# Splitting the routed experts' down weights once per expert, ahead of the expert loop, and taking their projection in fp32r

## The chip, the cores and the metric

One NeuronCore of a Trainium2 chip runs the whole kernel, as one program. The metric is the device time of one execution in microseconds (us). The kernel before takes 1118.25 us in the median of 3 runs (1118.01 to 1118.48).

## The reference, cut to what matters

```python
# B, S, D = 2, 1024, 512; T = B*S tokens; 16 heads of 32; 8 experts, inner width F = 352, top 2
def ref(x, Wq, Wk, Wv, Wo, router, bias, gate, up, down, sgate, sup, sdown):
    xn = layernorm(x)
    # causal attention, softmax, then the output projection
    Q, K, V = heads(xn @ Wq.T), heads(xn @ Wk.T), heads(xn @ Wv.T)
    A = softmax(where(causal, Q @ K.T / sqrt(32), -1e30)) @ V
    attn = merge(A) @ Wo.T
    # mixture of experts over the T tokens of xn: top 2 of 8, group-limited
    cw = combine_weights(sigmoid(xn @ router.T), bias)       # [T, 8], two non-zero per row
    routed = sum(cw[:, e:e+1] * (silu(xn @ gate[e].T) * (xn @ up[e].T)) @ down[e].T
                 for e in range(8))
    shared = (silu(xn @ sgate.T) * (xn @ sup.T)) @ sdown.T   # inner width 704
    return x + attn + routed + shared
```

## The kernel before, in words

Everything is float32. A product that is to be exact to float32 is taken in one of two ways. Either the operands stay float32, and each product takes two weight loads and two matmul records. Or each operand is split into a high part (a copy in fp32r) and a low part (the operand less its high part, again in fp32r), and three fp32r products are summed: high by high, high by low, low by high. All large products use the second way but one, the routed down projection.

The program is a sequence of blocks with a barrier between them:

1. `norm_phase` and `project_phase` (to about 210 us): layernorm, V, Q and K, the router.
2. `attend_phase` (to about 760 us): 32 heads (batch by head), each cut into 12 steps, written out in full (no loop on the chip). Every engine walks the same list of steps s = 0, 1, 2, ... and does for each step the stages whose lag fits. The scores for block s are taken at step s + 24 on TensorE (L1458), the exponential in the same step on ScalarE (`exp`, L1236) and its high part one step later (`hi`, L1243), the low part at step s + 26 (`lo`), on GpSimd for ten of a head's twelve blocks (L1198) and on VectorE for blocks 4 and 8 (L1325), and the product with V at step s + 30 (L1481, L1483). `prob` has four buffers, so `exp` of block s waits for `lo` of block s - 4; `ps_s` has two, so the scores of block s wait for `exp` of block s - 2. The shared expert's matmuls (L1514, L1539) are spread between the attention's as filler, so that every step has about equal TensorE work (`fill_counts`).
   SyncE (queue SP) loads for this phase in one loop over heads, `for g in range(HEADS + 4)`: `next_head(g)`, which first waits for the scores of head g - 4 and then issues 6 loads (L188, L190); for some g `load_xt` (one load of 2048 KB, L995; g = 3, 6, 11, 16, 20, 25, 30), or `store_acc` (4 stores of 256 KB, L1012) followed by `load_base` (L1006), which waits until those stores have landed and then issues 4 loads (g = 4, 8, 13, 17, 22, 27, 32; the first loads, at g = 1, have no store before them); then `load_values(g - 1)` (L989); then raw pieces of the shared expert's second half into `gu_raw` and `d_raw` (L1019 and the like, for g up to 15).
   GpSimd also works out where each token's row goes among the routed slots (`place()`: `expert_of`, `slot_table`), one small instruction a step.
3. `out_phase` (760 to 820 us): 16 token tiles, attention output by Wo, added to `out`. SP loads `wo` into the end of `d_sb`, a tile of `out` per step, and, at tiles 1 and 8, all weights of experts 0 and 1 with `load_expert` (L209, L212, L214).
4. `routed_phase` (820 us to the end): 39 tiles of 128 token slots, sorted by expert, so that an expert has some 5 tiles. On TensorE a tile j is worked on in three steps of a software pipeline, `pipeline(pe, NST, U, [(0, turn_x), (2, turn_h), (1, gate_up), (2, down)])`: transposes of the gathered rows (`ps_xt`, L1883), transposes of the hidden values of tile j - 2 (`ps_ht`, L1906), 24 fp32r matmuls for gate and up of tile j - 1 (L1895), and the down projection of tile j - 2 in float32 (L1916). ScalarE makes the high parts of the rows (L1797) and of the gate and up weights, once per tile and four chunks each (L1806), and the SiLU (L1819). VectorE makes the low parts (L1854, L1862), the hidden product (L1831), copies the transposed hidden values (L1839, L1841) and scales the result (L1847). GpSimd gathers rows (L1768) and adds results to `out` with an indirect DMA (L1779), one after the other. Each engine that needs the expert's number reads it with a load to a register (L1747). SP loads the remaining experts two ahead.

The change touches `attend_phase` (the SP loop, `place`, the GpSimd stream), `load_expert`, `out_phase` (where `wo` lies, the first loads) and `routed_phase` (all streams). New are `load_down`, `downs_loaded`, `load_down_raw`, `store_down_parts` and `split_down`.

## Time and profile before

| what | value |
|---|---|
| median of 3 runs | 1118.25 us |
| the profiled execution, its own time | 1127.01 us |
| span of the profiled execution (first to last instruction) | 1125.0 us |
| TensorE (PE) busy | 1046.2 us (93%) |
| VectorE (DVE) | 784.6 us (70%) |
| ScalarE (ACT) | 637.9 us (57%) |
| GpSimd (POOL) | 506.4 us (45%) |
| mean granted TensorE clock | 0.969 of full |
| DMA | 163.61 MB, mean 145 GB/s |

How to read it: the profile is of one execution, which took 8.8 us longer than the median of the runs without a profile. Busy time of PE counts modelled ends of pipelined matmuls; the pace of a run of matmuls is read from their starts. PEld is TensorE's weight load, which runs beside the matmuls.

### The profile page before, as it was taken

The page shows a single profiled execution, that of the slowest core. Times are in us where ns is not written, and L with a number is a line of the kernel's source. Part 1 is how long each engine was busy: PE and PEld are TensorE (multiplying, and loading weights), DVE is VectorE, ACT ScalarE, POOL GpSimd, SP SyncE. Part 2 cuts the span into 40 slices and gives each one's busy share as a digit, 9 for nine tenths or more (in the row PEclk, how much of TensorE's full clock was granted, in tenths as well). Part 3 has the DMA queues.
Part 4 walks back from the last instruction along what each step waited for, and adds up shares of the span by engine and source line. Part 5 has one row for each costly group of instructions (what it writes and reads, how often), then busy time and mean ns, then how long its engine had stood idle before and what let it go on. Part 6 is the DMA issues. An engine that isn't in the chain of part 4 may idle for free. (4 is left out here: it accounts for less than half of the span.)

```text
span 1125.0 us, 18890 instructions
## 1 busy us (share of the span) xinstructions
PE 1046.2 (93%) x5379; PEld 817.6 (73%) x5380; DVE 784.6 (70%) x1675; ACT 637.9 (57%) x1278; POOL 506.4 (45%) x568
## 2 busy tenths in 40 slices
PE   6999979888899998999999999998989999999994
PEld 4767867666677776777778777776867777778872
DVE  6732324565688887788888888865568888888872
ACT  3323211265588786787787887872155555565550
POOL 0013903388756564556566565651013443333321
PEclk9999989988899999999999999998989999999997
DMA  6989996255543553644445426118789444443432
GB/s 213 322 335 361 136 293 231 94 67 102 132 133 77 150 148 75 163 118 136 115 113 151 126 64 191 45 39 266 243 283 278 90 76 75 75 72 68 71 54 35
DMA packets 106201, 163.61 MB, mean 145 GB/s; under 512 B 53984, under 2 KB 64480, under 8 KB 102656
## 3 DMA queue, kind: packets, MB, share of 16 engines
q1 hardware_dynamic: 95776, 141.82, 44.1%
q0 software_dynamic: 9760, 20.49, 10.0%
q8 instruction: 38, 0.62, 0.2%
q14 instruction: 51, 0.42, 0.1%
q10 hardware_dynamic: 576, 0.26, 0.1%
HBM read 101.25 MB, written 61.28 MB: 144 GB/s over the span
## 5 line engine op out<-in xcount | busy, mean ns | idle before, releaser
L1198 POOL TENSOR_TENSOR prob_lo<-prob,prob_hi 128x512 fp32r<-128x512 f32 (+2 forms) x320 | 308.3, 977 | 203.3 <-ACT prob_hi L1243 147.0
L1236 ACT ACTIVATE prob<-ps_s 128x512 f32<-128x512 f32 (+3 forms) x384 | 188.0, 490 | 127.1 <-PE ps_s L1463 77.1
L1243 ACT ACTIVATE prob_hi<-prob 128x512 fp32r<-128x512 f32 (+3 forms) x384 | 198.6, 517 | 12.4 <-ACT row_stage L1217 12.4
L1862 DVE TENSOR_TENSOR rw_lo<-gu_sb,rw_hi 128x704 fp32r<-128x704 f32 x156 | 138.8, 893 | 52.7 <-ACT rw_hi L1806 47.7
L1306 DVE CUSTOM_DVE_ANT_0 ps_m<-ps_m,causal 128x384 f32<-128x384 f32 (+3 forms) x256 | 126.7, 495 | 69.2 <-PE ps_m L1432 66.9
L1806 ACT ACTIVATE rw_hi<-gu_sb 128x704 fp32r x156 | 123.5, 794 | 62.8 <-PE ps_ru L1895 43.6
L1458 PE MATMUL ps_s<-qs,ks 97*128 97x512 f32 (+3 forms) x384 | 140.4, 366 | 9.4 <-ACT prob L1236 9.2
L1779 POOL DMA_INDIRECT out<-work,slot_table x39 | 63.5, 1627 | 181.1 <-DVE work L1847 148.2
L1481 PE MATMUL ps_o<-prob_hi,vs 128*66 128x512 f32 (+3 forms) x384 | 133.1, 347 | 10.4 <-issue 9.6
L1432 PE MATMUL ps_m<-ks,qs 96*128 96x512 f32 (+3 forms) x384 | 139.1, 362 | 0.6 <-DVE maxima L1306 0.2
L1483 PE MATMUL ps_o<-prob_lo,vs 128*66 128x512 f32 (+3 forms) x384 | 132.0, 344 | 0.0
L1310 DVE TENSOR_REDUCE maxima<-ps_m 128x1 f32<-128x512 f32 x128 | 85.8, 682 | 41.5 <-PE ps_m L1432 40.4
L1916 PE MATMUL ps_ry<-d_sb,work 128*128 (+1 forms) x234 | 106.9, 593 | 1.2 <-issue 1.2
L1458 PEld LDWEIGHTS ps_s<-qs,ks 97*128 97x128 f32 x384 | 74.8, 195 | 30.8 <-ACT prob L1236 15.9
L1432 PEld LDWEIGHTS ps_m<-ks,qs 96*128 96x128 f32 x384 | 74.3, 193 | 23.6 <-DVE maxima L1306 4.6
L613 PE MATMUL ps_q<-xt,w_hi 128*128 128x512 f32 x256 | 82.0, 398 | 6.4 <-DVE work L725 6.4
L1481 PEld LDWEIGHTS ps_o<-prob_hi,vs 128*66 128x66 f32 x384 | 54.3, 141 | 32.1 <-issue 21.4
L725 DVE TENSOR_TENSOR work<-ps_q,work 128x512 fp32r<-128x512 f32 x32 | 21.8, 690 | 78.8 <-ACT work L574 76.9
L1514 PE MATMUL ps_f<-xt,sg_hi 128*128 128x512 f32 (+1 forms) x192 | 70.5, 400 | 3.8 <-PEq L496 2.7
L1514 PE MATMUL ps_f<-xt,su_hi 128*128 128x512 f32 (+1 forms) x192 | 71.5, 406 | 0.0
L1916 PEld LDWEIGHTS ps_ry<-d_sb,work 128*128 128x128 f32 (+1 forms) x234 | 43.4, 190 | 38.7 <-issue 38.7
L1768 POOL DMA_INDIRECT work<-xn_rows,slot_table x35 | 37.5, 1073 | 58.8 <-PE ps_xt L1883 48.7
(201 smaller groups left out, 2353.0 us busy)
## 6 DMA issues: line engine op xcount, KB each, us to landing
xt<-xt_blocks SPq DMA_DIRECT2D x7, 2048.0 KB, 9.1
v_rows<-work SPq DMA_DIRECT2D x16, 512.0 KB, 3.0
xt_blocks<-xt SPq DMA_DIRECT2D x4, 2048.0 KB, 11.3
qk_hi<-work SPq DMA_DIRECT2D x8, 1024.0 KB, 4.7
qk_lo<-work SPq DMA_DIRECT2D x8, 1024.0 KB, 7.5
qs<-qk_hi SPq DMA_DIRECT2D x64, 128.0 KB, 2.9
ks<-qk_hi SPq DMA_DIRECT2D x64, 128.0 KB, 3.2
vs<-v_rows SPq DMA_DIRECT2D x32, 256.0 KB, 4.7
```

The source lines that it names most:

```text
L1198: nc.gpsimd.tensor_tensor(prob_lo[:, s % NPL, 0:w], prob[:, s % NP, 0:w], prob_hi[:, s % NPH, 0:w].bitcast(F32), ALU.subtract).then_inc(lo ...
L1236: nc.scalar.activation(prob[:, s % NP, 0:w], ps_s[s % NS][:, 0:w], ACT.Exp, scale=SCALE).then_inc(exp_done, 1)
L1243: nc.scalar.activation(prob_hi[:, s % NPH, 0:w], prob[:, s % NP, 0:w], ACT.Copy).then_inc(hi_ready, 1)
L1306: nc.vector.tensor_tensor_reduce(ps_m[s % NM][:, 0:w], ps_m[s % NM][:, 0:w], causal[:, TBW - w:], 1.0, MASKED, ALU.add, ALU.max, maxima[:, ...
L1432: nc.tensor.matmul(ps_m[s % NM][:, 0:w], qs[0:ROWS, c, t * P:(t + 1) * P], ks[0:ROWS, c, k0:k0 + w], start=True, stop=True).then_inc(m_don ...
L1458: last = nc.tensor.matmul(ps_s[s % NS][:, 0:w], ks[0:ROWS + 1, c, kt * P:(kt + 1) * P], qs[0:ROWS + 1, c, q0:q0 + w], start=True, stop=not ...
L1481: nc.tensor.matmul(into, vs[:, c, kt, :], prob_hi[:, s % NPH, 0:w], start=n in STARTS, stop=False)
L1483: nc.tensor.matmul(into, vs[:, c, kt, :], prob_lo[:, s % NPL, 0:w], start=False, stop=n in ENDS).then_inc(pv_done, 1)
L1514: last = nc.tensor.matmul(ps_f[part][0:w, :], (w_hi, w_lo, w_hi)[term][:, kc, f0:f0 + w], xt[:, (0, 0, 1)[term], kc, :], start=(j == 0), s ...
L1806: nc.scalar.activation(w_hi[:, k, :], chunk(e, k), ACT.Copy).then_inc(w_hi_ready, 1)
L1862: nc.vector.tensor_tensor(w_lo[:, k, :], chunk(e, k), w_hi[:, k, :].bitcast(F32), ALU.subtract).then_inc(w_lo_ready, 1)
L1916: last = nc.tensor.matmul(ps_y[c % 2][:, :], hid_t[0:w, c % HR, k, :], d_sb[0:w, bass.ds(e * NF + k, 1), :].rearrange("p a d -> p (a d)"), ...
```

## The change

The down weights of the eight experts are cut into 24 pieces (8 experts by chunks of 128, 128 and 96 rows of 512). From head 18 of the SP loop on, two pieces a head (g = 18 to 29; `SPLIT_FROM` works out to 18) are loaded into `d_raw`; GpSimd makes the high part of each (a copy, into `gu_raw`) and the low part (a subtraction, in place), and SP stores both to a new DRAM tensor `down_split`. In the expert loop the split weights of an expert, twice as many bytes, are loaded into a ring of four places; the down projection takes nine fp32r matmuls a tile in place of three float32 ones; the hidden values are split on ScalarE (high) and VectorE (low); the scaling moves from VectorE to ScalarE. `place()` gets five more small instructions.

```diff
@@ attend_phase
+    SPLITS = E * NF
+    SPLIT_FROM = head_after(max(DOWN_SPLIT_AT) + 1)
+    MAKE_AT = {NB * (SPLIT_FROM + i // 2 - 1) + 5 + 3 * (i % 2): i for i in range(SPLITS)}
@@ SP
+                def load_down_raw(i):
+                    (e, k), n = divmod(i, NF), i % SR
+                    f0, w = FCH[k]
+                    if i < SR:
+                        sp.wait_ge(d_lo_ready, NF)
+                    wait(sp, parts_stored[n], stored_before + 32 * (i // SR))
+                    sp.dma_start(d_raw[0:w, n, :], down[e, f0:f0 + w, :]).then_inc(w_loaded[n], 16)
+                def store_down_parts(i):
+                    (e, k), n = divmod(i, NF), i % SR
+                    w = FCH[k][1]
+                    sp.wait_ge(down_made, 2 * i + 1)
+                    sp.dma_start(down_dram[e, 0:w, 0, k, :],
+                                 gu_raw[0:w, i % 2].rearrange("p k q -> p (k q)")
+                                 ).then_inc(parts_stored[n], 16)
+                    sp.wait_ge(down_made, 2 * i + 2)
+                    sp.dma_start(down_dram[e, 0:w, 1, k, :], d_raw[0:w, n, :]
+                                 ).then_inc(parts_stored[n], 16)
                 for g in range(HEADS + 4):
                     if HS <= g < HEADS:
                         next_head(g)
+                    i = 2 * (g - 1 - SPLIT_FROM)
+                    if 0 <= i < SPLITS:
+                        store_down_parts(i)
+                        store_down_parts(i + 1)
...
                         if g == DOWN_RAW_AT[k]:
                             load_shared_down(k)
+                    i = 2 * (g - SPLIT_FROM)
+                    if 0 <= i < SPLITS:
+                        load_down_raw(i)
+                        load_down_raw(i + 1)
@@ GpSimd
+                def split_down(s):
+                    if s in MAKE_AT:
+                        i = MAKE_AT[s]
+                        n, w = i % SR, FCH[i % NF][1]
+                        pool.wait_ge(w_loaded[n], raw_before + 16 * (i // SR + 1))
+                        if i >= 2:
+                            pool.wait_ge(parts_stored[(i - 2) % SR],
+                                         stored_before + 32 * ((i - 2) // SR + 1))
+                        into = gu_raw[0:w, i % 2].rearrange("p k q -> p (k q)")
+                        nc.gpsimd.tensor_copy(into.bitcast(F32R), d_raw[0:w, n, :]
+                                              ).then_inc(down_made, 1)
+                    if s - 1 in MAKE_AT:
...
+                        nc.gpsimd.tensor_tensor(d_raw[0:w, n, :], d_raw[0:w, n, :],
+                                                gu_raw[0:w, i % 2].rearrange("p k q -> p (k q)"),
+                                                ALU.subtract).then_inc(down_made, 1)
-                steps([(LO, lo)])
+                for s in range(max(ALL, max(MAKE_AT) + 2)):
+                    if 0 <= s - LO < STEPS:
+                        lo(s - LO)
+                    split_down(s)
@@ out_phase
-        wo_raw = d_sb[:, E * len(FCH) - KC:, :]
+        wo_raw = gu_sb[:, (E - 1) * KC:, 0:D]
-                        load_expert(sp, e, gate, up, down, gu_sb, d_sb, expert_loaded)
+                        load_expert(sp, e, gate, up, gu_sb, expert_loaded)
+                        load_down(sp, e, down_dram, d_ring, down_loaded)
@@ routed_phase, SP: experts 4 to 7 of the ring
+                for e in range(DOWN_SLOTS, E):
+                    first = sp.value_load(first_of[0:1, e - DOWN_SLOTS + 1:e - DOWN_SLOTS + 2],
+                                          min_val=1, max_val=NST + 1)
+                    sp.wait_ge(y_ready, first)
+                    load_down(sp, e, down_dram, d_ring, down_loaded)
+                    sp.wait_ge(down_loaded[e % DOWN_SLOTS], downs_loaded(e))
+                    sp.sem_inc(downs_ready, 1)
@@ routed_phase, ScalarE
+                def hidden_hi(i, c):
...
+                    nc.scalar.activation(hid_hi[:, c % HR, 0:2, :], ps_h[:, 0:2, :], ACT.Copy
+                                         ).then_inc(h_hi_ready, 1)
+                    nc.scalar.activation(hid_hi[0:w, c % HR, 2, :], ps_h[0:w, 2, :], ACT.Copy
+                                         ).then_inc(h_hi_ready, 1)
+                def weigh(i, c):
...
+                    nc.scalar.activation(y[:, c % R, :], ps_y[c % 2][:, :], ACT.Copy,
+                                         scale=slot_table[:, bass.ds(j, 1), 1]).then_inc(y_ready, 1)
-                pipeline(act, NST, U, [(0, turn_x), (0, first_chunks), (1, gate_unit), (0, last_chunk)],
+                pipeline(act, NST, U, [(0, turn_x), (3, weigh), (2, hidden_hi), (0, first_chunks),
+                                       (1, gate_unit), (0, last_chunk)], back=R)
@@ routed_phase, VectorE
+                def hidden_lo(i, c):
...
+                    nc.vector.tensor_tensor(hid_lo[:, c % HR, 0:2, :], ps_h[:, 0:2, :],
+                                            hid_hi[:, c % HR, 0:2, :].bitcast(F32), ALU.subtract)
+                    nc.vector.tensor_tensor(hid_lo[0:w, c % HR, 2, :], ps_h[0:w, 2, :],
+                                            hid_hi[0:w, c % HR, 2, :].bitcast(F32), ALU.subtract)
-                pipeline(dve, NST, U, [(4, turn_h), (2, x_lo), (2, first_chunks),
-                                       (3, hidden), (2, last_chunk), (4, weigh)], back=U)
+                pipeline(dve, NST, U, [(0, x_lo), (2, hidden_lo), (0, first_chunks),
+                                       (1, hidden), (0, last_chunk)], back=U)
@@ routed_phase, TensorE
                 def down(i, c):
                     e = expert(pe, j)
-                    pe.wait_ge(experts_ready, e + 1)
+                    n = pe.value_load(down_slot[0:1, bass.ds(j, 1)], min_val=0,
+                                      max_val=DOWN_SLOTS - 1)
+                    pe.wait_ge(downs_ready, e + 1)
                     wait(pe, h_ready, 2 * (j + 1))
-                    wait(pe, y_ready, j - 1)
+                    wait(pe, y_ready, j)
                     for k, (f0, w) in enumerate(FCH):
-                        last = nc.tensor.matmul(
-                            ps_y[c % 2][:, :], hid_t[0:w, c % HR, k, :],
-                            d_sb[0:w, bass.ds(e * NF + k, 1), :].rearrange("p a d -> p (a d)"),
-                            start=(k == 0), stop=(k == NF - 1))
+                        for of, part in ((hid_hi, 0), (hid_hi, 1), (hid_lo, 0)):
+                            last = nc.tensor.matmul(
+                                ps_y[c % 2][:, :], of[0:w, c % HR, k, :],
+                                d_ring[0:w, bass.ds(n, 1), part * NF + k, :]
+                                .rearrange("p a d -> p (a d)"),
...
```

## Rows read from the trace of the kernel before

**Rows 1.** Windows, a head and the loop: us, busy PE PEld DVE ACT POOL, PEclk, DMA.

```profile
613.07:628.55 15.48, 15.48 (x90) 12.43 (x89) 12.81 (x35) 12.41 (x28) 9.49 (x11) 1.00 0.31 69
...
830.00:1125.00 295.00, 277.96 (x1417) 219.18 (x1415) 221.74 (x343) 160.26 (x227) 98.51 (x72) 0.98 0.48 101
```

**Rows 2.** Chain of waits, one tile of the expert loop: start us, us, what.

```profile
1003.34 2.58 PE ps_ry L1916 x6
1005.92 0.44 PE ps_xt L1883 x4
...
1010.56 0.86 PE ps_ry L1916 x2
```

**Rows 3.** Timeline of ACT and DVE in that tile: start us, us, instruction.

```profile
1011.48 0.52 DVE L1831 TENSOR_TENSOR work<-ps_ru,work 128x352 f32<-128x352 f32 x1
1011.55 0.79 ACT L1806 ACTIVATE rw_hi<-gu_sb 128x704 fp32r x1 [0.49 <-issue]
```

**Rows 4.** Timeline of PE in the output projection, eight matmuls apart.

```profile
785.17 0.39 PE L1697 MATMUL ps_ay<-wo_hi,a_hi 128*128 128x512 f32 x1
...
787.01 0.39 PE L1697 MATMUL ps_ay<-wo_hi,a_lo 128*128 128x512 f32 x1
```

**Rows 5.** Groups by form of POOL: busy us, mean ns | idle before.

```profile
L1198 POOL TENSOR_TENSOR prob_lo<-prob,prob_hi 128x512 fp32r<-128x512 f32 x128 | 166.3, 1312 | 68.9 <-ACT prob_hi L1243 67.3 <-PE ps_o L1483 0.4
...
L705 POOL CAST sd_hi<-sd_raw 96x512 fp32r<-96x512 f32 x1 | 0.7, 671 | 0.0
```

**Rows 6.** Groups by form of DVE, one that reads two SBUF operands.

```profile
L1352 DVE TENSOR_TENSOR o_sum<-o_part 128x128 f32<-128x128 f32 x64 | 41.1, 643 | 0.0
```

**Rows 7.** Timeline of POOL, blocks 2 and 3, then 5, of the head at 628.55.

```profile
634.96 1.44 POOL L1198 TENSOR_TENSOR prob_lo<-prob,prob_hi 128x384 fp32r<-128x384 f32 x2 [0.67 <-ACT prob_hi L1243]
638.77 0.74 POOL L1198 TENSOR_TENSOR prob_lo<-prob,prob_hi 128x256 fp32r<-128x256 f32 x1 [2.37 <-ACT prob_hi L1243]
```

**Rows 8.** Timeline of ACT and PE: exponential of block 9, scores of block 11.

```profile
641.71 0.28 ACT L1236 ACTIVATE prob<-ps_s 128x128 f32<-128x128 f32 x1 [0.34 <-PE ps_s L1463]
...
643.97 0.45 PE L1458 MATMUL ps_s<-qs,ks 97*128 97x512 f32 x1
```

**Rows 9.** Timeline of SP's issues in two heads.

```profile
597.86 0.31 SPq L188 DMA_DIRECT2D qs<-qk_hi  x1
...
601.81 0.43 SPq L989 DMA_DIRECT2D vs<-v_rows  x1
...
628.55 0.30 SPq L188 DMA_DIRECT2D qs<-qk_hi  x1
...
638.01 0.43 SPq L989 DMA_DIRECT2D vs<-v_rows  x1
```

**Rows 10.** Line L989, window 601 to 603: its DMA to landing.

```profile
DMA to landing us min/median/max: 8.8/8.8/8.8
```

**Rows 11.** Line L989, window 638 to 638.5: its DMA to landing.

```profile
DMA to landing us min/median/max: 4.7/4.7/4.7
```

**Rows 12.** Line L989, the eight heads from 516 to 645: DMA to landing.

```profile
DMA to landing us min/median/max: 3.7/4.3/10.5
```

**Rows 13.** Line L1012, four stores of 256 KB of one head.

```profile
L1012 SPq DMA_DIRECT2D out<-y_acc x4: 422/442/461, 631.2 to 632.7; - x4
...
DMA to landing us min/median/max: 3.1/3.4/3.5
```

**Rows 14.** Timeline of ACT, then PE, around a late raw piece of `gu_raw`.

```profile
445.32 0.52 ACT L1277 ACTIVATE sg_hi<-gu_raw 128x384 fp32r<-128x384 f32 x1 [1.80 <-DMA gu_raw<-in_sup]
...
447.62 0.42 PE L1481 MATMUL ps_o<-prob_hi,vs 128*66 128x512 f32 x1 [2.75 <-issue]
```

**Rows 15.** Windows, columns as in rows 1: that head, and 3.4 us in it.

```profile
435.80:455.40 19.60, 16.85 (x90) 13.33 (x88) 14.53 (x37) 13.28 (x30) 9.49 (x11) 0.91 0.34 75
...
448.00:451.40 3.40, 3.40 (x15) 2.74 (x14) 1.54 (x3) 1.32 (x4) 1.72 (x2) 0.50 0.00 0
```

**Rows 16.** Timeline of DVE in the output projection.

```profile
778.68 0.69 DVE L1665 TENSOR_TENSOR y_tile<-ps_ay,y_tile 128x512 f32<-128x512 f32 x1 [2.31 <-DMA y_tile<-out]
```

More of the change, by code:

```diff
@@ L210, in load_expert, with downs_loaded, load_down @@
                       src[e * KC:(e + 1) * KC].rearrange("k p f -> p k f")).then_inc(loaded, 16)
-    at = len(FCH) * e
-    eng.dma_start(d_sb[:, at:at + 2, :], down[e, 0:2 * P, :].rearrange("(k p) d -> p k d", p=P)
-                  ).then_inc(loaded, 16)
-    eng.dma_start(d_sb[0:FCH[-1][1], at + 2, :], down[e, 2 * P:F, :]).then_inc(loaded, 16)
+def downs_loaded(e):
+    n = e % DOWN_SLOTS
+    raw = 16 * E * len(FCH) // DOWN_RAW if n < DOWN_RAW else 0
+    return W_BEFORE + raw + 64 * (e // DOWN_SLOTS + 1)
+def load_down(eng, e, down_dram, d_ring, down_loaded):
+    n, w = e % DOWN_SLOTS, FCH[-1][1]
+    for part in range(2):
+        at = part * len(FCH)
+        eng.dma_start(d_ring[:, n, at:at + 2, :].bitcast(F32), down_dram[e, :, part, 0:2, :]
+                      ).then_inc(down_loaded[n], 16)
+        eng.dma_start(d_ring[0:w, n, at + 2, :].bitcast(F32), down_dram[e, 0:w, part, 2, :]
+                      ).then_inc(down_loaded[n], 16)
 def norm_phase(nc, x, wv, wqk, xt, w_raw, w_loaded, ident, v_dram, xn_dram, out, work, v_stored,
@@ L780, in attend_phase @@
                  shared_w, sgate, sup, sdown, chosen, weight, earlier_of, count_of, slot_of, entry,
[L781 removed]
+                 slot_table, expert_of, down_slot, first_of, down, down_dram, slots_dram, out,
+                 attended, qk_stored, xt_stored, w_loaded, parts_stored):
     HS = HEAD_SLOTS
```

112 lines of the change are left out of this document (79 added, 33 removed).

## The prediction

> **What bounds the kernel now.** I read the windows by stage first, then the chain of waits in the last stage, then the timelines around the two places that the change touches. The reader is to see two stages in which TensorE is never idle. In the attention phase an ordinary head takes 15.48 us and PE is busy for all of it; DVE, ACT and POOL have 2.7, 3.1 and 6.0 us to spare [rows 1]. Whatever makes PE wait there is paid in full. In the expert loop the chain runs on PE alone: a tile's down projection takes 2.58 us, and the next begins 7.22 us after it [rows 2]. So PE time saved there is gained in full too, until another engine becomes the bound.
>
> **The gain: nine fp32r matmuls for three float32 ones.** The down projection of a tile is 2.58 us on the chain (six records) [rows 2]. An fp32r matmul of 128x512, one after the other, starts every (787.01 - 785.17) / 8 = 0.230 us in the output projection [rows 4]; its operands have the same shapes, and 96 rows in place of 128 change no columns. Nine are 2.07 us, so a tile saves 0.51. The end hangs on the down of the last tile but one (the last scatter waits for the one before it), so 38 of the 39 tiles count: -19.4. I take off 0.5 for the second register read that TensorE's sequencer gets: **-18.9 us**. Bounds: nothing, if another engine takes over as the bound (below), and -20.
>
> Does ACT or DVE take over? The new period is 7.22 - 0.51 = 6.71. ACT is busy 160.26 of 295 us [rows 1], 3.9 a tile; it gets the scaling (at most the 0.79 of a 704-wide one [rows 3]) and two copies (0.28 is the price of a 128-wide one [rows 8]; twice as wide, about 0.4), 1.5 in all, and stands still 0.49 for a register read [rows 3], perhaps now twice: 6.4. It fits by 0.3. DVE loses the scaling and its two copies become two subtractions: 221.74 of 295 is 5.4 a tile now and falls. The tightest wait: the hidden product ends at 1012.00, which is 6.1 after its tile's start at 1005.92 [rows 2, 3]; ACT's new work ahead of the weight chunks may put it off by 0.7, to 6.8, and PE needs it for the transposes at 6.71 + 0.44. It fits too. SP's added loads here (split weights of 1408 KB for 704 KB an expert, every five tiles) have whole tiles to land: 0.
>
> **The cost that decides: GpSimd stands in line with what PE needs.** The split adds 24 copies and 24 subtractions to POOL, two of each in the heads after SP's g = 18 to 29. A copy is 0.67, a subtraction 1.31 [rows 5], together 4.0 a head against 6.0 spare [rows 1]; the place of the first is well chosen, a gap of 2.37 us behind block 3 [rows 7]. The work itself costs nothing there. The wait ahead of the copy can: POOL waits until the raw piece has landed, and queued behind it on POOL are the low parts of blocks 5, 6 and 7. `exp` of block 9 waits for the low part of block 5, the scores of block 11 wait for that `exp`, and PE does nothing past them.
>
> I count from the first issue of a head on SP. POOL is free for the copy at 634.96 + 1.44 - 628.55 = 7.9; the scores of block 11 start at 643.97 - 628.55 = 15.4 [rows 7 to 9]. From the landing L of the piece to the end of that `exp` it is 0.67 + 1.31 + 0.74 + 0.28 = 3.0 [rows 5, 7, 8]. So PE stands still for L - 12.4, if that is above zero.
>
> L is read from `load_values`, which is now the last load of a head; the raw load is issued just behind it. Ahead of both, the change puts four stores of up to 256 KB. Four such stores land between 631.2 + 3.1 and 632.7 + 3.5, so 1.9 / 3 = 0.6 apart, 2.5 for four [rows 13]; the raw piece adds 0.6. L is the old landing of the values + 3.1.
> - Eight heads have nothing else on the queue: issue some 3 after the head's first, landing 3.7 to 4.3 later [rows 12], L is about 10: late for POOL by 2, early for PE by 2. Cost 0.
> - At g = 20 and 25 the 2048 KB of `xt` stand ahead. The values of g = 25 are issued at 601.81 and land 8.8 later, 12.8 after the head's first issue [rows 9, 10]: L = 15.9, PE waits 3.5. The other one took 10.5 to land [rows 12]; I count 1 more for it, 4.5.
> - At g = 22 and 27 SP first waits for four stores of `y_acc` to land, then issues four loads. The values of g = 27 are issued at 638.01 and land 4.7 later, at 14.2 [rows 9, 11]: L = 17.3, PE waits 4.9. Twice, 9.8.
>
> Together **+17.8 us**. Bounds: if the stores cost nothing ahead (they run beside the rest), each L is 2.5 less, and the four waits come to 7.8; if the stores land as slowly as the slowest values do, 6 more in all.
>
> The trace has a small case of this: ACT waits 1.80 us for a late piece of `gu_raw`, and PE stands still for 2.75 [rows 14]. Then the clock is granted at 0.50 for 3.4 us, and that head takes 19.60 [rows 15]. 2.75 idle and 1.7 lost at half the clock (1.2 for 2.4 GHz) make 4.4 of the 4.1 us that it is longer than an ordinary one. The four new waits are all longer than 2.75, so each brings the 1.7: **+6.8** (0 if the clock stays up).
>
> **Output projection.** Experts 0 and 1 bring 704 KB more on SP's queue, in two more issues each. The third tile of `out` already lands late: DVE waits 2.31 for it, until 778.68 [rows 16]. At 0.6 us per 256 KB the added bytes are 1.7 us, and that tile and those behind it shift by as much; I take +1.5. Below 0 nothing here can save; above it I allow 4, for the slower pace that the queue shows when several loads stand on it [rows 12].
>
> **Everything else.** The scaling moved to ACT at the end of the kernel: one instruction on the chain on either engine, 0. Five small POOL instructions in `place()`, one a step, beside work: 0. The last stores of pieces are at g = 30, long before the phase ends: 0.
>
> **Sum.** -18.9 + 17.8 + 6.8 + 1.5 = +7.2. Against the profiled execution, 1125.0 of span and 2.0 around it, that gives 1134.2; the median of the runs lies 8.8 below the profiled one, and I carry the difference over: 1118.25 + 7.2 = **1125.5 us**.
>
> **A rule of the skill against the change.** A DVE subtraction of 128 columns with both operands in SBUF takes 643 ns in the mean [rows 6], more than the 520 of a product over 352 columns with one operand in PSUM [rows 3]. POOL is at work in most of that time. The Trainium skill, SBUF — State Buffer, section Who interferes with whom, says that a DVE instruction with two SBUF inputs and a GpSimd instruction that reads SBUF shut each other out for a whole instruction; by that rule the trace agrees, and the 48 new POOL instructions each could hold DVE up. It is the fourth rival.
>
> **Rivals.**
> 1. *POOL's wait is absorbed (faster).* If the raw pieces don't queue behind `xt`, or the engines have more in hand than I count, the attention phase costs little and the loop's gain stands: 1118.25 - 18.9 + 1.5 = 1101; with half of my 17.8 and no slow clock, 1110. For it: POOL is idle for 6 us a head, ten of twelve heads lose nothing by my own count. Against: the values behind `xt` landed 8.8 and 10.5 after their issue, against 3.7 at best [rows 10, 12]; and where SP stands waiting for stores, the raw load isn't even issued. It turns to the forecast where L passes 12.4. Chance 0.27.
> 2. *The loop gains nothing.* ACT's chain gets longer than 6.71 and takes the bound: the gain falls to a few us or nothing, and with the costs the time is about 1140. The margin is 0.3 us. Chance 0.07.
> 3. *The pieces are split, but the change only moves the time about:* stalls and gain cancel to within a few us, 1116 to 1120. It needs stalls of just about 15 to 19. It lies inside the forecast's spread.
> 4. *The shared port.* 3.9 us of new POOL work a head could hold DVE for as long; it has 2.7 to spare after an ordinary head [rows 1], so up to 1.3 a head, 12 heads, 15 us on top: 1141. For it rows 6; against: DVE's instructions that PE waits for read PSUM. Chance 0.04.
>
> **How the numbers follow.** The forecast's case has 0.62, the rivals 0.27, 0.07 and 0.04. Its own range is 1112 (transfers beside each other, part of the slow clock) to 1138 (slow stores). The range to be given reaches down to rival 1 and leaves out the worst of 2 and 4: 1101 to 1138. A measurement of this kernel tells 0.2%, 2.2 us, from no change. Faster: all of rival 1 and a small part of the forecast's spread, 0.30; within: 0.06; slower: 0.64.
>
> **What would show it.** Right: in the loop, nine records for the down projection 0.23 apart and a period of 6.7; in the attention phase four heads (g = 20, 22, 25, 27) 5 to 7 us longer, each with PE idle for 3 to 5 us before the scores of a block 11, POOL's copy ending its idle time on the raw piece's DMA, and a granted clock of 0.5 behind it; the other eight heads as before. Wrong: POOL's copy never waits long, or POOL waits and PE's idle time in the attention phase stays as it is (then rival 1); a period above 6.9 (rival 2); all twelve heads longer by an equal bit (rival 4). If ordinary heads also show PE waits, I took their L too early.

## The result

The changed kernel takes **1157.83 us** (median of 4 runs, 1148.54 to 1161.1) beside 1118.13 for the kernel before (4 runs, 1113.33 to 1118.48): ratio 1.0354, 95% interval 1.0297 to 1.0411. The direction was forecast, the size was not: 1125.5 us, range 1101 to 1138.

### The profile after

The profiled execution has a span of 1154.9 us. First the windows by stage: attention from its first scores to its last, the output projection, the expert loop. The columns are those of [rows 1]. The same stages of the kernel before last 534.5, 59.5 and 304.5 us.

```profile
220.00:804.50 584.50, 524.24 (x2790) 402.63 (x2789) 449.61 (x1045) 400.43 (x910) 391.72 (x408) 0.95 0.48 132
812.00:872.60 60.60, 55.25 (x256) 44.48 (x257) 29.39 (x52) 12.00 (x20) 3.90 (x4) 0.92 0.82 264
872.60:1154.90 282.30, 262.91 (x1560) 244.43 (x1560) 202.93 (x312) 201.16 (x352) 104.30 (x74) 0.98 0.56 132
```

Attention is 50.0 us longer, the output projection 1.1, the loop 22.2 shorter; with 1.1 ahead of attention that is the difference of 29.9 us between the two profiled executions. The medians are 39.7 apart, since the profiled execution of before stood 8.8 above its median and this one stands 1.2 below its own. Where the time of attention goes, one window shows, over the twelve heads from the scores that begin with SP's g = 19 up to those that begin with its g = 31, before and after:

```profile
504.60:692.90 188.30, 185.88 (x1054) 146.18 (x1054) 159.93 (x406) 149.67 (x340) 115.78 (x120) 1.00 0.45 124
```
```profile
505.20:744.10 238.90, 201.65 (x1054) 153.94 (x1054) 181.99 (x407) 148.14 (x340) 161.77 (x164) 0.92 0.55 168
```

The same PE instructions take 50.6 us more; the other heads are unchanged in sum. PE is idle for 37.3 us of the window where it was for 2.4, and busy for 15.8 us more, while the mean clock falls from 1.00 to 0.92 of 2.4 GHz. Of the 50.6 us, 32.9 are in the four heads of the forecast (g = 20, 22, 25 and 27, longer by 7.1 to 10.2 each); the other eight, forecast to stay as they were, are longer by 1.1 to 5.7 each. VectorE, whose work there did not change, is busy for 22 us more: that is the first sign of the rival (the shared port) to which the forecast had given a chance of 0.04.

The loop answers to [rows 2]: nine records for the down projection, 6.67 us from one tile to the next.

```profile
888.37 2.09 PE ps_ry L2060 x9
895.04 2.09 PE ps_ry L2060 x9
```

The waits of attention in the changed kernel (who waited for whom: us in total, times, longest). None of these four had a counterpart in the same heads before:

```profile
POOL gu_raw L1297 <- DMA d_raw<-in_down: 47.5, 10, 11.1
...
ACT prob L1343 <- POOL prob_lo L1283: 31.3, 11, 9.0
...
PE ps_o L1588 <- ACT o_copy L1359: 24.8, 7, 8.9
...
PE ps_m L1539 <- DVE maxima L1417: 7.2, 3, 3.9
```

Two kinds of stall are in it. **The first**, in the head of g = 22. SP's timeline (start, us, instruction) from the head's first issue:

```profile
563.06 0.33 SPq L198 DMA_DIRECT2D qs<-qk_hi  x1
...
568.20 3.02 SPq L1049 DMA_DIRECT2D out<-y_acc  x4
574.44 1.76 SPq L1043 DMA_DIRECT2D y_acc<-out  x4
576.25 0.43 SPq L1026 DMA_DIRECT2D vs<-v_rows  x1
576.73 1.07 SPq L1070 DMA_DIRECT2D d_raw<-in_down  x2
```

and the timelines of GpSimd, ScalarE and PE:

```profile
582.50 0.61 POOL L1297 CAST gu_raw<-d_raw 96x512 fp32r<-96x512 f32 x1 [11.06 <-DMA d_raw<-in_down]
583.18 1.26 POOL L1303 TENSOR_TENSOR d_raw<-d_raw,gu_raw 96x512 f32<-96x512 f32 x1
```
```profile
585.24 0.28 ACT L1343 ACTIVATE prob<-ps_s 128x128 f32<-128x128 f32 x1 [8.99 <-POOL prob_lo L1283]
...
586.45 0.58 ACT L1359 ACTIVATE o_copy<-ps_o 66x512 f32<-66x512 f32 x1
```
```profile
577.32 0.45 PE L1565 MATMUL ps_s<-qs,ks 97*128 97x512 f32 x1
...
587.08 0.69 PE L1588 MATMUL ps_o<-prob_hi,vs 128*66 128x512 f32 x1 [8.85 <-ACT o_copy L1359]
```

The copy starts as soon as the piece has landed, L = 582.50 - 563.06 = 19.4 us after the head's first issue, and PE stands still for 8.85 us, not before the scores of block 11 but a step earlier: at the V product of block 4, the first into `ps_o` for the second half, which needs ScalarE's `o_copy` of the first half. That copy stands on ScalarE behind the `exp` of block 9, and that `exp` is what waits for GpSimd.

**The second kind** follows the second piece of g = 28, whose first one came at L = 11.4, later than GpSimd could have begun but without the long wait of the four heads. GpSimd and VectorE:

```profile
703.79 1.28 POOL L1303 TENSOR_TENSOR d_raw<-d_raw,gu_raw 128x512 f32<-128x512 f32 x1
705.03 5.30 POOL L1283 TENSOR_TENSOR prob_lo<-prob,prob_hi 128x128 fp32r<-128x128 f32 x5
```
```profile
703.40 2.22 DVE L1432 TENSOR_TENSOR prob_lo<-prob,prob_hi 128x512 fp32r<-128x512 f32 x1
705.54 0.42 DVE L1413 CUSTOM_DVE_ANT_0 ps_m<-ps_m,causal 128x256 f32<-128x256 f32 x1
705.88 0.14 DVE L1413 DVE_READ_ACCUMULATOR2_ANT maxima<- 128x1 f32 x1
706.06 4.30 DVE L1421 TENSOR_TENSOR maxima<-maxima 128x4 f32<-128x4 f32 x1
```

A maximum over 128x4 elements takes 4.30 us; in the kernel before, the 32 of this form take 0.16 to 1.10. It has two inputs in SBUF. GpSimd works through five low parts without a pause, and VectorE's instruction ends at 710.36, when GpSimd's last one does (710.33). The reduction before it (L1413), with an input in PSUM, takes 0.42. PE waits 3.92 us for the maxima behind. VectorE's instructions over 1.9 us in this phase: four, 13.9 us in all; before the change there was none.

### The profile page after: what moved, and what is told of

Read it like the earlier page. It is cut to its first block and busy times, and to the rows that moved or that the text cites. A ratio compares the mean times of both kernels' runs of the same rounds, so it can differ in the third digit from the quotient of the medians.

```text
span 1154.9 us, 19715 instructions
## 1 busy us (share of the span) xinstructions
PE 1038.8 (90%) x5496; PEld 842.2 (73%) x5497; DVE 784.3 (68%) x1636; ACT 671.7 (58%) x1395; POOL 561.3 (49%) x621
## 5 line engine op out<-in xcount | busy, mean ns | idle before, releaser
L1283 POOL TENSOR_TENSOR prob_lo<-prob,prob_hi 128x512 fp32r<-128x512 f32 (+2 forms) x320 | 311.9, 988 | 153.4 <-ACT prob_hi L1350 113.6
L1350 ACT ACTIVATE prob_hi<-prob 128x512 fp32r<-128x512 f32 (+3 forms) x384 | 198.7, 518 | 12.4 <-ACT row_stage L1324 12.0
L1413 DVE CUSTOM_DVE_ANT_0 ps_m<-ps_m,causal 128x384 f32<-128x384 f32 (+3 forms) x256 | 126.4, 494 | 80.9 <-PE ps_m L1539 77.9
L1588 PE MATMUL ps_o<-prob_hi,vs 128*66 128x512 f32 (+3 forms) x384 | 135.6, 353 | 36.0 <-ACT o_copy L1359 24.8
L2003 DVE TENSOR_TENSOR rw_lo<-gu_sb,rw_hi 128x704 fp32r<-128x704 f32 x156 | 135.6, 891 | 35.9 <-ACT rw_hi L1935 34.3
L1539 PE MATMUL ps_m<-ks,qs 96*128 96x512 f32 (+3 forms) x384 | 141.7, 369 | 11.2 <-DVE maxima L1417 7.2
L1565 PEld LDWEIGHTS ps_s<-qs,ks 97*128 97x128 f32 x384 | 76.1, 198 | 30.2 <-ACT prob L1343 11.3
L2060 PE MATMUL ps_ry<-d_ring,hid_t_hi 128*128 (+1 forms) x234 | 73.3, 394 | 1.7 <-DVE hid_t_lo L1988 1.7
L1897 POOL DMA_INDIRECT work<-xn_rows,slot_table x35 | 40.1, 1147 | 61.1 <-PE ps_xt L2024 51.1
L599 ACT ACTIVATE work<-ps_q 128x512 fp32r<-128x512 f32 x32 | 18.8, 599 | 75.4 <-PE ps_q L638 53.7
```

What stands on the lines that cost most here:

```text
L1283: nc.gpsimd.tensor_tensor(prob_lo[:, s % NPL, 0:w], prob[:, s % NP, 0:w], prob_hi[:, s % NPH, 0:w].bitcast(F32), ALU.subtract).then_inc(lo ...
L1350: nc.scalar.activation(prob_hi[:, s % NPH, 0:w], prob[:, s % NP, 0:w], ACT.Copy).then_inc(hi_ready, 1)
L1413: nc.vector.tensor_tensor_reduce(ps_m[s % NM][:, 0:w], ps_m[s % NM][:, 0:w], causal[:, TBW - w:], 1.0, MASKED, ALU.add, ALU.max, maxima[:, ...
L1539: nc.tensor.matmul(ps_m[s % NM][:, 0:w], qs[0:ROWS, c, t * P:(t + 1) * P], ks[0:ROWS, c, k0:k0 + w], start=True, stop=True).then_inc(m_don ...
L1565: last = nc.tensor.matmul(ps_s[s % NS][:, 0:w], ks[0:ROWS + 1, c, kt * P:(kt + 1) * P], qs[0:ROWS + 1, c, q0:q0 + w], start=True, stop=not ...
L1588: nc.tensor.matmul(into, vs[:, c, kt, :], prob_hi[:, s % NPH, 0:w], start=n in STARTS, stop=False)
```

## The experiments

The column "12 heads" of the table is the same window in each run, beside 188.3 before and 238.9 after. "Held" counts VectorE's instructions over 1.9 us there, with their sum. "Outside" is the span less that window. A median is compared by its ratio to the kernel before on the same chip, with the 95% interval. The runs e1 to e4 were taken on one chip, e5 to e7, e8 to e10, and e11 with e12 on others, where the kernel before had medians of 1120.5 to 1122.0 us; so a difference between the medians of two runs of different groups carries some us of that.

```
run                    us median  ratio [interval]          12 heads  held       outside
after                  1157.83    1.0354 [1.0297, 1.0411]   238.9     4, 13.9    916.0
e2_no_split            1106.14    0.9869 [0.9831, 0.9906]   188.2     0          917.0
e3_pool_only           1107.14    0.9889 [0.9851, 0.9927]   191.2     0          912.0
e4_dma_only            1140.15    1.0179 [1.0139, 1.0218]   222.4     0          916.2
e1_raw_first           1123.88    1.0022 [0.9992, 1.0052]   206.4     3, 10.5    915.6
e5_head_ahead          1110.49    0.9916 [0.9888, 0.9943]   193.6     1, 2.3     915.9
e6_copy_o_first        1148.43    1.0255 [1.0204, 1.0305]   235.2     5, 15.9    913.3
e7_three_later         1149.97    1.0273 [1.0218, 1.0328]   236.1     8, 29.4    912.5
e8_pool_only_later     1133.81    1.0120 [1.0085, 1.0154]   218.3     7, 24.2    911.1
e9_pool_copies_twice   1115.16    0.9954 [0.9929, 0.9979]   200.7     2, 4.0     912.1
e10_act_copies         1114.29    0.9938 [0.9915, 0.9961]   199.4     0          915.4
e11_no_max_of_maxima   1133.31    1.0099 [1.0070, 1.0128]   215.6     7, 20.8    919.8
e12_both_free_steps    1111.81    0.9908 [0.9873, 0.9944]   191.4     0          915.7
```

### Four runs that take the split apart

**e2_no_split**: the new loop, no split; the raw loads of pieces and the stores of parts go too, and `down` itself is passed in place of `down_dram`, and loaded as both parts, so the down projection computes something else.

```diff
-                    split_down(s)
...
-        eng.dma_start(d_ring[:, n, at:at + 2, :].bitcast(F32), down_dram[e, :, part, 0:2, :]
+        eng.dma_start(d_ring[:, n, at:at + 2, :].bitcast(F32),
+                      down_dram[e, 0:2 * P, :].rearrange("(k p) d -> p k d", p=P)
```

> No split in attention at all (no raw loads, no POOL copies and subtractions, no stores); the routed loop is that of the change, and loads the raw down weights as both parts, so its output is not the reference's. Theory: attention is as before the change and the loop keeps its 22 us gain, 1094 to 1100 us. Rival (the loop gains only because something was taken over from attention): 1105 to 1120 us.

Measured: 1106.14 us. Attention falls back to that of before, to 0.1 us in the twelve heads. From its first to its last matmul the loop takes 268.9 us, as in the changed kernel, against 290.3. The output projection takes 62.7 us against 59.4. The ratio puts the gain at 10.5 to 19 us; the profiles give -21.4 + 3.3 = -18.1. The median lies above the 1094 to 1100 that I expected, and in the range of the rival. The rival's mechanism isn't it: attention is as before, and the loop gains all the same. The output projection's share makes 3.3 us of the miss, and the median of the kernel before, 2 us higher on this chip, another 2.

**e3_pool_only**: e2 plus all of GpSimd's work, on three pieces loaded once.

```diff
+                    if g == SPLIT_FROM - 1:
+                        for i in range(SR):
+                            load_down_raw(i)
...
-                        if i >= 2:
-                            pool.wait_ge(parts_stored[(i - 2) % SR],
-                                         stored_before + 32 * ((i - 2) // SR + 1))
```

> POOL does all 24 copies and 24 subtractions at their places, on three pieces that are loaded once a head before, so that it waits for no DMA; no stores; the loop as in the run without a split, raw weights as both parts, so its output is not the reference's. Theory (lateness is the cost, not the work): within 5 us of the run without a split. Rival A (POOL's work and the port that it shares with DVE cost the time): 15 to 45 us above it, spread evenly over the 12 heads.

**e4_dma_only**: the changed kernel, with each copy and subtraction cut to 8 columns.

```diff
-                        nc.gpsimd.tensor_copy(into.bitcast(F32R), d_raw[0:w, n, :]
+                        nc.gpsimd.tensor_copy(into[:, 0:8].bitcast(F32R), d_raw[0:w, n, 0:8]
```

> All loads, stores and waits of the split as in the changed kernel, but POOL's copies and subtractions take 8 columns each, so the stored parts are not the down weights and the output is not the reference's. Theory: the same four heads stall at the V product of block 4 by 1 to 2 us less each, and the backlog behind them is gone: attention 25 to 35 us above that of before, 1120 to 1132 us. Rival A (POOL's work is the cost): attention as before, 1097 to 1105 us.

Measured: the twelve heads take 188.2 us without a split, 191.2 with the work alone, 222.4 with the transfers alone, 238.9 with both. So the work costs 3 us when nothing makes it late (as expected of e3), the late transfers 34, and the two together 13.5 more than their sum. By medians it is 1.0, 34.0 and 16.7, the last across two chips. The expectation of e4 (25 to 35 us) held in attention; its total came out 8 us above the range, which had the loop's gain too large. PE's waits in e4 that aren't there before are one kind only (but for one of 0.3), and four times, at g = 20, 22, 25 and 27:

```profile
PE ps_o L1588 <- ACT o_copy L1359: 24.7, 4, 8.2
```

The changed kernel has 24.8 us of this wait, as much. What it has on top is PE waiting for VectorE's maxima, 9.6 us in all against 0.3 in e4.

**e1_raw_first**: the two raw loads ahead of `xt` and `y_acc` on SP's queue.

```diff
                         store_down_parts(i + 1)
+                    i = 2 * (g - SPLIT_FROM)
+                    if 0 <= i < SPLITS:
+                        load_down_raw(i)
+                        load_down_raw(i + 1)
...
-                    i = 2 * (g - SPLIT_FROM)
-                    if 0 <= i < SPLITS:
-                        load_down_raw(i)
-                        load_down_raw(i + 1)
```

> The two raw loads of a head stand ahead of the shared experts' loads on SP's queue, with everything else as in the changed kernel. Theory (POOL's copies come late in the four heads whose raw loads stand behind an xt load or the four stores and loads of y_acc, PE stops at the V product of block 4, and POOL's backlog then holds up the rest): the four heads fall back to the time of the others, some 45 of the 50 us that attention lost come back, 1102 to 1115 us. Rival A (POOL's own work and the shared port cost the time, whatever the loads do): 1140 to 1158 us. Rival B (the xt and y_acc loads, now 4 to 5 us later, are what PE waits for instead): 1120 to 1140 us, with PE idle at the shared experts' products.

Measured: 1123.88 us, above the expected range and in that of rival B, whose sign (PE idle at the shared expert's products) is missing: PE waits there for 1.6 us, as in e3. 34 of the 51.7 us that the changed kernel lies above e2 come back, not 45. L falls to 7.8 to 10.9 in ten of the twelve heads with a piece and GpSimd's longest wait for a piece to 4.1 us. But the three instructions held on VectorE cost some of it. In the head after a wait of 3.05 us (g = 23) VectorE's timeline reads

```profile
584.74 4.62 DVE L1491 TENSOR_TENSOR hid_lo<-hid,hid_hi 128x512 fp32r<-128x512 f32 x1
589.29 0.42 DVE L1413 CUSTOM_DVE_ANT_0 ps_m<-ps_m,causal 128x256 f32<-128x256 f32 x1
```

with PE idle for 4.02 us behind it, while GpSimd does four low parts in a row. A small lateness is enough to start it.

### Is it the step that I named, and the way PE stops?

**e6_copy_o_first**: ScalarE's `o_copy` one step earlier, ahead of the `exp`.

```diff
-                    for lag, stage in ((COPY, copy_o), (EXP, exp), (ROW + 1, row), (HI, hi),
+                    for lag, stage in ((COPY - 1, copy_o), (EXP, exp), (ROW + 1, row), (HI, hi),
```

> As the changed kernel, but ScalarE copies ps_o of a first half one step earlier, ahead of block 9's exp instead of behind it. Theory (PE stops at the V product of block 4 because that copy stands behind an exp that waits for POOL): those stops go, PE runs on until the scores of block 11 as the prediction had it, a step of 1.3 to 1.5 us less in each of the four heads, so 4 to 12 us less than the changed kernel, 1145 to 1153 us. Rival (the copy itself was not what PE waited for): 1155 to 1160 us. Should ScalarE now stall on the V product in every head, some us are lost over all 32.

Measured: 1148.43 us, 9 less, within the expectation; in the twelve heads of the two profiled executions the difference is 3.7 us. The stop moves to where the prediction had it, the scores:

```profile
574.37 0.80 PE L1565 MATMUL ps_s<-qs,ks 97*128 97x512 f32 x1 [6.75 <-ACT prob L1343]
```

L is 19.0, 17.6 and 18.4 us at g = 22, 25 and 27, PE's stops are 6.75, 4.95 and 6.57. L less the stop is 12.3, 12.7 and 11.8, against the 12.4 of the prediction. In the changed kernel L less the stop is 10.7, 10.6 and 11.3 at g = 20, 22 and 25 (stops of 6.15, 8.85 and 5.39). At g = 20 of e6 (L = 17.3) the stop is only 1.65, after two waits for VectorE's maxima of 1.3 each.

**e5_head_ahead**: a fourth place, each piece loaded a head before its copy. (`before`, a scratch tile of the placement, moves into that place, which is free until then.)

```diff
-DOWN_RAW = 3
+DOWN_RAW = 4
...
-    MAKE_AT = {NB * (SPLIT_FROM + i // 2 - 1) + 5 + 3 * (i % 2): i for i in range(SPLITS)}
+    MAKE_AT = {NB * (SPLIT_FROM + i // 2) + 5 + 3 * (i % 2): i for i in range(SPLITS)}
...
-                    i = 2 * (g - 1 - SPLIT_FROM)
+                    i = 2 * (g - 2 - SPLIT_FROM)
```

> A fourth place for the raw pieces, each loaded a head before its copy, the loads left behind xt and y_acc on SP's queue; the same work, the same transfers. Theory (late raw loads are the whole cost): POOL waits for no raw piece, attention falls to that of the run with POOL's work alone, 534 to 545 us, and the kernel takes 1104 to 1114 us, faster than before by some 1%. Rival B (the 24 loads and 48 stores themselves, by SP's queue or by the DMA engines, delay xt, y_acc and the values): 1118 to 1130 us, with PE idle for shared products or V products that wait for a load. Rival A (port) is left only where POOL works without a pause.

Measured: 1110.49 us, as expected, ratio 0.9916 [0.9888, 0.9943], faster than before by 0.6 to 1.1%. The transfers are all there, and their share of the DMA engines' time is larger than before and after:

```profile
502.20:695.80 193.60, 188.60 (x1054) 146.65 (x1053) 171.54 (x406) 148.74 (x340) 162.44 (x168) 0.99 0.68 203
```

So bytes and SP's queue cost PE little but by making a piece late: the twelve heads take 2.4 us more than with GpSimd's work alone (e3). Rival B is out.

### Place, pauses, and the held instructions

**e7_three_later** and **e8_pool_only_later** make the same edit, e7 on the changed kernel, e8 on e3.

```diff
-    MAKE_AT = {NB * (SPLIT_FROM + i // 2 - 1) + 5 + 3 * (i % 2): i for i in range(SPLITS)}
+    MAKE_AT = {NB * (SPLIT_FROM + i // 2 - 1) + 8 + 3 * (i % 2): i for i in range(SPLITS)}
```

> As the changed kernel, but POOL takes each piece three steps (some 3.9 us) later in its order. Theory (a race between the raw load and the copy's place in POOL's order): each stall shrinks by 3.9 us, from 6.2, 8.9, 5.4 and 2.1 us to 2.3, 5.0, 1.5 and 0, the backlog behind them goes, and attention stands 12 to 25 us above before, 1112 to 1132 us. Rival C (SP waits three steps longer before its stores and stands ahead of xt and y_acc with that wait, so the loads come later by as much as the copy): 1145 to 1165 us. Rival A (POOL's work): unchanged, 1150 to 1160 us.

> POOL's 24 copies and 24 subtractions with no raw load or store to wait for, as before, but three steps later in its order (the output is not the reference's: raw weights as both parts). Theory (VectorE's instructions with two inputs in SBUF are held up only while POOL works off a backlog that a late load has made): within 5 us of the run with POOL's work at its old place, 1103 to 1112 us, and no such instruction over 2 us. Rival (the place is what counts: three steps later the subtraction falls beside VectorE's o_sum and maxima work): 1118 to 1135 us, with instructions of 3 to 5 us in most of the 12 heads.

The theory failed in both. e7 gave 1149.97 us where I had 1112 to 1132. GpSimd's wait for raw pieces did shrink, from 47.5 us to 17.3, but eight instructions of VectorE were held, 29.4 us in all, and PE waits 19.2 us for the maxima of L1413. The time is in the range of rival C, but that rival (loads later by as much as the copy) explains one stop of PE: behind a raw piece that was 7.0 us late for GpSimd, with PE idle for 4.05. e8 has no transfer to be late for and takes 1133.81 us, 26.7 above e3: the theory "late transfers only" was too narrow, and the rival that the place counts has the number. What differs between e3 and e8 is seen in the groups by form of VectorE, first of e3, then of e8 (busy us, mean ns; window 500:735 in both, which goes on past the twelve heads):

```profile
L1412 DVE TENSOR_TENSOR maxima<-maxima 128x4 f32<-128x4 f32 x14 | 9.6, 684 | 0.5
L1482 DVE TENSOR_TENSOR hid_lo<-hid,hid_hi 128x512 fp32r<-128x512 f32 x7 | 6.5, 922 | 1.0 <-ACT hid_hi L1366 1.0
L1408 DVE TENSOR_REDUCE maxima<-ps_m 128x1 f32<-128x512 f32 x56 | 37.4, 681 | 8.9 <-PE ps_m L1530 8.4
```
```profile
L1412 DVE TENSOR_TENSOR maxima<-maxima 128x4 f32<-128x4 f32 x14 | 16.6, 1187 | 0.5
L1482 DVE TENSOR_TENSOR hid_lo<-hid,hid_hi 128x512 fp32r<-128x512 f32 x5 | 7.8, 1552 | 0.0
L1408 DVE TENSOR_REDUCE maxima<-ps_m 128x1 f32<-128x512 f32 x53 | 35.3, 681 | 11.7 <-PE ps_m L1530 11.4
```

The two forms with both inputs in SBUF go from 684 to 1187 and from 922 to 1552 ns (in the twelve heads alone from 575 to 1203 and from 940 to 1552); the reduction that reads PSUM stays at 681. The timelines of GpSimd and VectorE in e8 show one case:

```profile
585.47 1.07 POOL L1288 CAST gu_raw<-d_raw 96x512 fp32r<-96x512 f32 x1
586.50 1.29 POOL L1277 TENSOR_TENSOR prob_lo<-prob,prob_hi 128x512 fp32r<-128x512 f32 x1
587.75 1.26 POOL L1294 TENSOR_TENSOR d_raw<-d_raw,gu_raw 96x512 f32<-96x512 f32 x1
588.98 2.93 POOL L1277 TENSOR_TENSOR prob_lo<-prob,prob_hi 128x512 fp32r<-128x512 f32 x2
```
```profile
585.99 4.79 DVE L1482 TENSOR_TENSOR hid_lo<-hid,hid_hi 128x512 fp32r<-128x512 f32 x1
```

The later place puts a copy and a subtraction between the 512 wide low parts of a head's last blocks and the next head's first, so GpSimd has five such instructions in a row. At the old place the first subtraction falls in the step whose low part is VectorE's, where GpSimd has nothing else.

**e9_pool_copies_twice**: e3, each copy done twice.

```diff
...
+                        nc.gpsimd.tensor_copy(into.bitcast(F32R), d_raw[0:w, n, :]
+                                              ).then_inc(down_first, 1)
+                        pool.wait_ge(down_first, i + 1)
                         nc.gpsimd.tensor_copy(into.bitcast(F32R), d_raw[0:w, n, :]
```

> POOL's work alone with nothing to wait for, at its old place, but each copy done twice, so that POOL is asked for some 2 us more in a head and works nearly without a pause (the output is not the reference's: raw weights as both parts). Theory (VectorE is held when POOL leaves no pause, whatever the reason): instructions of 2 to 5 us on VectorE now appear with no late transfer at all, and the time is 8 to 40 us above the 1107 us of the run with single copies. Rival (only a late transfer makes it): 1104 to 1112 us.

Measured: 1115.16 us, 8.0 above e3, at the lower end. VectorE's busy time in the twelve heads rises from 168.3 to 179.7 us, with two instructions of just under 2.0 and none longer, where I had expected some of 2 to 5. PE waits 6.0 us for maxima, eleven times, against 0.8 in e3. Less of a pause on GpSimd costs time with no transfer involved, but more work at a good place costs far less than the same work at a bad one.

**e11_no_max_of_maxima**: e8 without the 128x4 maximum.

```diff
-                        nc.vector.tensor_tensor(maxima[:, c, 4:QT], maxima[:, c, 4:QT],
-                                                maxima[:, c, QT:QT + 4],
-                                                ALU.max).then_inc(max_ready, 1)
+                        dve.sem_inc(max_ready, 1)
```

> The run with POOL's work alone, three steps later (1134 us), with one more thing left out: VectorE's maximum of the two halves' maxima (128x4 from two inputs in SBUF), which took 4.4 and 5.0 us in two heads there with PE idle behind it; its semaphore is still raised. The output is not the reference's. Theory (an instruction of VectorE with two inputs in SBUF is held while POOL runs without a pause, one that reads PSUM is not): without it VectorE goes on to the reductions that PE waits for, and the two stalls of 3.1 and 3.5 us with their slow clock go, 1119 to 1128 us. Rival (the hold passes to the next instruction of that kind, prob_lo, before PE is served, or PE is short of something else): 1130 to 1137 us.

Measured: 1133.31 us, no gain: the rival. Seven instructions are held again, 20.8 us, three of them `o_sum` (2.69 to 2.88 us), and PE still stands 3.2 us behind VectorE's maxima. The hold isn't bound to one instruction: the next one with two SBUF inputs takes it.

**e10_act_copies**: e5, the copies on ScalarE.

```diff
+                        nc.scalar.activation(into.bitcast(F32R), d_raw[0:w, n, :],
+                                             ACT.Copy).then_inc(down_hi, 1)
```

> The version with a fourth place and loads a head ahead, but the 24 copies are done by ScalarE (0.6 us each), so POOL only subtracts. Theory (what is left of the cost is POOL's thin slack): the last 3 to 5 us of attention come back, 1104 to 1110 us. Rival (ScalarE's exps are closer to PE's path than POOL's subtractions): 1112 to 1125 us, with PE idle before scores on ACT prob in the 12 heads.

Measured: 1114.29 us, in the range of the rival, and no better than e5. No instruction is held, but the twelve heads take 199.4 us against 193.6. The rival's sign, PE idle before scores, isn't there: PE stands still for 0.46 to 1.16 us in each of the twelve heads, ahead of the V product of block 0. On ScalarE the copy stands ahead of the `o_copy` that this product needs (they start at 573.85 and 574.39 in one head, the product at 575.06).

**e12_both_free_steps**: e5, the second piece one step later.

```diff
-    MAKE_AT = {NB * (SPLIT_FROM + i // 2) + 5 + 3 * (i % 2): i for i in range(SPLITS)}
+    MAKE_AT = {NB * (SPLIT_FROM + i // 2) + 5 + 4 * (i % 2): i for i in range(SPLITS)}
```

> The version with a fourth place and loads a head ahead, with the second piece one step later, so that both subtractions fall in steps whose prob_lo is VectorE's and POOL has nothing else. Theory (POOL's pauses decide): the remainder in the 12 heads (some 5 us) falls, 1104 to 1110 us beside some 1110. Rival (the remainder is noise and the y_acc wait): the same within 2 us.

Measured: 1111.81 us, ratio 0.9908 [0.9873, 0.9944]: by the median the rival, the same within 2 us. In the profiled execution the twelve heads take 191.4 us, 2.2 less than in e5, and nothing is held; the medians can't tell the two apart. Both e5 and e12 are faster than the kernel before and the changed one.

## Why the prediction was right in direction and wrong in size

**The gain of the loop was right.** Nine products take 2.09 us, 0.232 each (forecast 0.230), and the period is 6.67 to 6.68, against 6.71. Forecast -18.9, measured -21.4 from the loop's first to its last matmul (18.6 to 21.4 less over all versions with this loop). ScalarE, busy for 201 of 282 us, does not become the bound; rival 2 is out.

**The output projection was about right**: forecast +1.5, measured +1.1 in the profile of the changed kernel and +3.3 in that of e2, one profiled execution each.

**The cost of attention was forecast at 17.8 + 6.8 = 24.6 us and came to 50.6.** The long stalls are in the four heads forecast, by the race forecast; three of the four are longer than forecast. PE stands still for 24.8 us behind `o_copy`, where 17.8 were forecast, and for 9.6 behind VectorE's maxima, where nothing was; the slower clock makes most of the rest, some 13 us against 6.8. Three terms of the sum were off, and a fourth was put at nothing:

```
g    L forecast  L measured   stall forecast  stall measured
20   16.9        16.9         4.5             6.15
22   17.3        19.4         4.9             8.85
25   15.9        16.7         3.5             5.39
27   17.3        18.2         4.9             2.13, and 3.00 before it, behind maxima
```

- *The slack.* The step "the scores of block 11 wait for that `exp`, and PE does nothing past them" failed. PE meets the V product of block 4 first, a step earlier, because `o_copy` stands on ScalarE behind the same `exp`. The slack is 10.6 to 11.3 us, not 12.4. e6, where `o_copy` goes ahead, gives back the forecast's stop and its slack (11.8 to 12.7).
- *L at g = 22.* I took the issue of the values at g = 27, 9.5 us after the head's first issue [rows 9], for g = 22 as well. In the kernel before they are issued at 11.0 there, and land 4.8 later:

```profile
551.29 0.30 SPq L188 DMA_DIRECT2D qs<-qk_hi  x1
...
562.28 0.43 SPq L989 DMA_DIRECT2D vs<-v_rows  x1
```

  With my 3.1 for the stores and the piece that makes 18.9, against 19.4 measured. The term for the stores was about right: the values of g = 22 and 27 are issued 2.2 and 2.9 us later than in the same heads before, where I charged 2.5.
- *The clock.* I gave each stall one stretch of 3.4 us at 0.50, 1.7 us lost. The changed kernel has seven stretches between 541 and 736 us, 37.5 us in all. PE is busy for 26.9 us of them, so about half of that, 13.4 us, is lost; the other 10.6 pass while it stands still. Half the clock also follows stalls that weren't forecast.

With the transfers alone (e4) the cost is 34 us, where the forecast's stalls and clock came to 24.6.

**The cause that I left out of the sum, with a chance of 0.04, brings the rest.** Rival 4, the shared port, was set aside because the instructions of VectorE that PE waits for read PSUM. They do, and they keep their 681 ns; but they queue behind one that does not. (The instruction of [rows 6], read there as a subtraction, is the addition of `o_sum`; it has two inputs in SBUF all the same.) It is not a tax on every head, as the rival had it (all twelve heads by 1.3 us): the work on time costs 3 us in twelve heads (e3). It bites where GpSimd has no pause, which a late piece brings about, since all that was queued behind it is then worked off in one go (13.5 to 16.7 us on top), and which a bad place brings about without any late piece (e8, 27 us). By the rule of the Trainium skill that the prediction cited (SBUF — State Buffer, Who interferes with whom) a loser blocks for one whole instruction of the other engine. The kernel before agrees with it: its 128x4 maxima take at most 1.10 us, less than the 1.31 of one subtraction of GpSimd [rows 5]. That a blocked instruction stays blocked through four or five of them, here 4.30 to 5.00 us, is what the runs add. "The work itself costs nothing there" was true only of the work in time. That the port is what holds VectorE is argued from that page and from which instructions are held (all of those over 1.9 us in the twelve heads, in every run, have two inputs in SBUF); no run takes the port away while GpSimd works.

**The range.** Rivals 1 and 3 asked whether the waits would be absorbed; nothing among my cases made the stalls and the port act together, so the range ended at 1138 (the bounds that I gave, 6 for slow stores and 2.5 for the output projection, reach only 1134). The difference of 8.8 us between the profiled execution and its median, which I carried over, was not a constant of the kernel: it was 1.2 the other way after.

What stays open: how much of the slow clock belongs to which kind of stall; and why the output projection, up to the loop's first matmul, lies between 60.3 and 64.6 us from one version to the next, where TensorE's code is the same. Neither was tried.

## What to carry to other kernels

When a step with a DMA behind it is put into the in-order stream of an engine, ask three things of it: how late the transfer can be in the worst head (issue times of the queue, not bytes alone), which is the *first* instruction of the bound engine that hangs on anything queued behind it (follow every engine's own order, copies that look unrelated too), and what the engine does while it catches up. Loaded a whole head ahead, the same work and bytes that cost some 52 us here cost 4 to 5 (both against e2). GpSimd's idle share said little here about what it can take: keep pauses in it, and place its work where VectorE has no instruction with two SBUF inputs that the bound engine waits behind.

## What the hardware showed that I had not expected

- VectorE's instruction of 128x4 elements took 4.30 us in the changed kernel and 5.00 in e8, and one of 128x512 4.62 in e1 and 4.79 in e8 (0.92 in the mean of e3), each while GpSimd ran instruction after instruction; the reductions that read PSUM kept their mean of 681 ns in e3 and e8.
- In e8 the instruction of 4.79 us ended at 590.78, not at the end of a row of GpSimd's work but within it: there one low part of GpSimd took 1.71 us instead of 1.26. So the held instruction got in at last, and GpSimd waited for it. This is no exception: of the 19 held instructions of the changed kernel, e7 and e8, 14 ended while GpSimd went on without a pause. What lets one in was not tried.
- Doing 24 loads and 48 stores more in twelve heads raised the DMA share from 0.45 to 0.68 (e5), and the heads took 2.4 us more than in the run with GpSimd's work alone (3.4 by the medians, on two chips).
